# Expert blocks of 128 tokens: 28 tiles of two blocks, then 15 tiles of one block, in a fused two-layer attention and expert kernel

## The reference

```python
# layer 0: E, F, K = 8 experts, 1024 hidden, top 2
probs = softmax(x @ router_w.T); top_w, top_idx = top_k(probs, 2)
top_w = top_w / (sum(top_w) + 1e-9)
h = relu(x @ w1[e].T + b1[e]); y = h @ w2[e].T + b2[e]
out = sum over the two chosen experts of top_w * y
# layer 1: 8 experts, 512 hidden, top 2
h = silu(x @ w1[e]) * (x @ w2[e]); y = h @ w3[e]
out = sum over the two chosen experts of top_w * y
```

## Time and profile before

| | us |
|---|---|
| median of 3 runs | 1743.08 (1738.2 to 1744.42) |
| the profiled execution's own time | 1736.38 |
| its span, first to last instruction | 1734.7 |
| mean granted TensorE clock | 0.927 of 2.4 GHz |
| PE busy | 1543.9 (89%) |
| DVE, ACT, POOL busy | 1095.6, 836.8, 739.2 |

### The profile page before, as it was taken

How to read it: one execution, slowest core, us unless ns; L and a number is a source line. 1 busy time by engine, 2 the same in 40 slices (tenths; PEclk the granted TensorE clock), 3 DMA queues, 4 the chain that set the end, 5 groups by cost and what they waited for, 6 DMA issues and landing times. The chain is left out here.

```text
span 1734.7 us, 38336 instructions
## 1 busy us (share of the span) xinstructions
PE 1543.9 (89%) x12676; PEld 1149.2 (66%) x12676; DVE 1095.6 (63%) x1913; ACT 836.8 (48%) x1548; POOL 739.2 (43%) x521
## 2 busy tenths in 40 slices
PE   7798898897988679999999997999978589999996
PEld 2433334334337568888888885777768579999996
DVE  5687687687778824555554443888868834454443
ACT  2664755655634335555554441666754322322321
POOL 3501303205100036666665442777760046666664
PEclk8899899899895789999999998899995789999999
DMA  6411312213207264555553224200007154443443
GB/s 188 135 56 56 118 61 87 82 61 109 73 25 268 96 232 117 143 144 139 143 145 65 48 44 100 62 25 25 26 2 239 65 159 65 66 68 62 63 65 46
DMA packets 105122, 163.65 MB, mean 94 GB/s; under 512 B 10896, under 2 KB 70340, under 8 KB 104708
## 3 DMA queue, kind: packets, MB, share of 16 engines
q1 hardware_dynamic: 72247, 117.98, 20.8%
q0 software_dynamic: 29952, 40.91, 14.1%
q10 hardware_dynamic: 2791, 2.84, 0.5%
HBM read 92.91 MB, written 68.79 MB: 93 GB/s over the span
## 5 line engine op out<-in xcount | busy, mean ns | idle before, releaser
L1322 PE MATMUL e_ph<-e_zTt,weights_a 128*128 128x256 f16 x3744 | 424.8, 274 | 2.3 <-issue 2.0
L1322 PEld LDWEIGHTS e_ph<-e_zTt,weights_a 128*128 x3744 | 364.6, 98 | 54.0 <-issue 10.7
L1272 POOL DMA_INDIRECT e_zt<-token_parts,slot_token x156 | 172.0, 1103 | 210.3 <-issue 201.9
L1450 DVE TENSOR_TENSOR e_hl<-e_h,e_hh 128x512 f16<-128x512 f32 x156 | 104.4, 690 | 212.0 <-ACT e_hh L1414 189.1
L1400 ACT ACTIVATE e_h<-e_ph,e_b 128x256 f32<-128x256 f32 x312 | 130.6, 470 | 215.6 <-PE e_ph L1322 137.2
L1282 POOL DMA_INDIRECT token_rows<-e_ysb,slot_token x78 | 158.6, 2034 | 173.8 <-DVE e_ysb L1477 159.4
L1336 PE MATMUL e_pyt<-weights_b,e_hh 128*128 x1248 | 210.7, 273 | 0.6 <-DVE e_ysb L1477 0.6
L704 ACT ACTIVATE probs<-lower_banks,shift 128x1024 f32<-128x1024 f32 x128 | 137.3, 1112 | 90.7 <-PE lower_banks L578 89.2
L1282 POOL DMA_INDIRECT out_dram<-e_ysb,slot_token x78 | 124.4, 1595 | 109.2 <-DVE e_ysb L1481 86.5
L1336 PE MATMUL e_pyt<-weights_b,e_hl 128*128 x624 | 170.1, 273 | 0.0
L739 DVE TENSOR_TENSOR acc<-acc,probs 128x1024 f32<-128x1024 f32 (+1 forms) x112 | 136.8, 1222 | 23.6 <-ACT probs L704 20.3
(11 more groups left out here) (233 smaller groups left out, 2867.6 us busy)
## 6 DMA issues: line engine op xcount, KB each, us to landing
weight_parts<-w_split SPq DMA_DIRECT2D x32, 512.0 KB, 3.3
weights_a<-weight_parts SPq DMA_DIRECT2D x16, 1024.0 KB
x_sb<-in_u SPq DMA_DIRECT2D x24, 512.0 KB
weight_parts<-x_sb SPq DMA_DIRECT2D x24, 512.0 KB
w_raw<-in_w1T SPq DMA_DIRECT2D x16, 512.0 KB, 4.5
w_raw<-in_w2T SPq DMA_DIRECT2D x16, 512.0 KB, 4.8
weights_b<-weight_parts SPq DMA_DIRECT2D x8, 1024.0 KB
token_parts<-x_sb SPq DMA_DIRECT2D x8, 1024.0 KB, 5.3
```

Source lines behind the costliest of these rows:

```text
L1272: pool.indirect_dma_start(zt[:, i % 2, c, :], None, g.zrows, at).then_inc(ld[i % 2], 16)
L1322: last = pe.matmul(ph[:, q, f, :], up_w(wp, e, k, 2 * q + f), zTs[:, i % 2, 2 * zp + k, :], start=(n == 0), stop=(n == 5))
L1450: dve.tensor_tensor(hl[:, s, 2 * q:2 * q + 2, :], src[:, q % 2], hh[:, s, 2 * q:2 * q + 2, :], ALU.subtract).then_inc(lo_done, 1)
```

## The change

Each expert's run is padded to 128 slots. `BLOCKS = (2*B*S + E*(P-1)) // P` = 71 blocks stand in place of 78. `PAIRS = 28` tiles of two blocks come first (each expert's even part), then 15 tiles of one block (the odd blocks and what is left), `NT` = 43. `extent(i)` gives a tile's first block, its number of blocks and how many hidden blocks share a PSUM bank.

- A tile of one block makes the same 48 up matmuls, with 128 columns instead of 256, into two banks (alternating between the two halves of `ph`), 4 transposes instead of 8, and one `down` instead of two.
- Its up weights come from `own_w`, two fixed buffers of 1 MB in the upper part of the x buffer. SP's `fetch_own(i)` reads the tile's expert and copies both parts from `weight_parts`. The first two are issued behind `bring_home`, ahead of layer 0's first two `fetch`; each later one waits for the up of the tile two before.
- ACT and DVE work on units of 4 x 128 columns. In layer 0 a unit is four activations of 128 columns. ACT's second loop ends at tile 28, DVE's loop at tile 26; the tiles behind are written out.
- `route` has more steps: pairs and odd blocks are counted and scanned apart, and the expert of each tile comes from two comparisons. One-hot rows shrink from 78 to 71 blocks.

```diff
-NT = (2 * B * S + E * (C * P - 1)) // (C * P)
+BLOCKS = (2 * B * S + E * (P - 1)) // P
+PAIRS = (2 * B * S // P - E) // C
+NT = PAIRS + BLOCKS - C * PAIRS
...
-            step(dve.tensor_scalar(cnti[:], ptot[:, 0:E], float(C * P - 1), None, ALU.add))
-            step(dve.tensor_scalar(cntj[:], cnti[:], (C * P).bit_length() - 1, None, ALU.logical_shift_right))
-            step(dve.tensor_copy(cnt[:], cntj[:]))
-            step(dve.tensor_tensor_scan(cumt[:], g.ones[:, 0:E], cnt[:], 0.0, ALU.mult, ALU.add))
-            step(dve.tensor_tensor(base[:], cumt[:], cnt[:], ALU.subtract))
-            step(dve.tensor_scalar(base[:], base[:], float(C * P), None, ALU.mult))
-
-            step(dve.tensor_tensor(lg[:], prk[:, 0:T * E].rearrange("p (t e) -> p t e", e=E), over_t(base[:]), ALU.add))
+            step(dve.tensor_scalar(cnti[:], ptot[:, 0:E], float(P - 1), None, ALU.add))
+            step(dve.tensor_scalar(blocksi[:], cnti[:], P.bit_length() - 1, None, ALU.logical_shift_right))
+            step(dve.tensor_scalar(pairsi[:], blocksi[:], 1, None, ALU.logical_shift_right))
+            step(dve.tensor_scalar(oddi[:], blocksi[:], 1, None, ALU.bitwise_and))
+            step(dve.tensor_copy(pairs[:], pairsi[:]))
+            step(dve.tensor_copy(odd[:], oddi[:]))
+            step(dve.tensor_tensor_scan(cum_pairs[:], g.ones[:, 0:E], pairs[:], 0.0, ALU.mult, ALU.add))
+            step(dve.tensor_tensor_scan(cum_odd[:], g.ones[:, 0:E], odd[:], 0.0, ALU.mult, ALU.add))
+            step(dve.tensor_scalar(limit[:], pairs[:], float(C * P), None, ALU.mult))
+            step(dve.scalar_tensor_tensor(base[:], cum_pairs[:], float(C * P), limit[:], ALU.mult, ALU.subtract))
+            step(dve.tensor_scalar(away[:], cum_pairs[:], cum_pairs[:, E - 1:E], float(-C * P), ALU.subtract, ALU.mult))
+            step(dve.tensor_tensor(odd[:], cum_odd[:], odd[:], ALU.subtract))
+            step(dve.scalar_tensor_tensor(away[:], odd[:], float(P), away[:], ALU.mult, ALU.add))
+            ranks = prk[:, 0:T * E].rearrange("p (t e) -> p t e", e=E)
+            step(dve.tensor_tensor(wk2, ranks, over_t(limit[:]), ALU.is_ge))
+            step(dve.tensor_tensor(wk2, wk2, over_t(away[:]), ALU.mult))
+            step(dve.tensor_tensor(lg[:], ranks, over_t(base[:]), ALU.add))
+            step(dve.tensor_tensor(lg[:], lg[:], wk2, ALU.add))
...
+            def fetch_own(i):
+                s, b = i % 2, i + PAIRS
+                if i >= PAIRS + 2:
+                    sp.wait_ge(up_done, UB * b - UB)
+                e = expert_of(sp, i)
+                sp.dma_start(own_w[:, s], g.parts[layer][:, :, bass.ds(e, 1), 0:2 * F0].rearrange("p w o n -> p w (o n)")
+                             ).then_inc(own_ld[s], 16)
...
+                if single:
+                    pe.wait_ge(own_ld[s], 16 * ((i - PAIRS) // 2 + 1))
                 pe.wait_ge(zev, i + 1)
-                for q in range(Q):
+                for q in range(UB * cols):
+                    bank = UB * s + q if single else q
...
-                                last = pe.matmul(ph[:, q, f, :], up_w(wp, e, k, 2 * q + f), zTs[:, i % 2, 2 * zp + k, :],
+                                last = pe.matmul(out[:, f, :], up_of(i, e, wp, k, per * q + f), zTs[:, s, 2 * zp + k, 0:cols * P],
...
-                down(i, 0, e[i])
-                if i + 2 < NT:
-                    e[i + 2] = expert_of(pe, i + 2)
-                down(i, 1, e[i])
+                for c in range(extent(i)[1]):
+                    if c == extent(i)[1] - 1 and i + 2 < NT:
+                        e[i + 2] = expert_of(pe, i + 2)
+                    down(i, c, e[i])
```

More of the change, by code:

```diff
@@ L1190, in experts @@
     NF = F // P
[L1191 to L1194, removed]
+    UB = 2
+    HB = UB if layer == 0 else 1
     KINDS = 3
@@ L1233, in experts, with extent, place, landed @@
         up_w, down_w = g.up_w, g.down_w
+        def extent(i):
+            if i < PAIRS:
+                return C * i, C, 2
+            return i + PAIRS, 1, 4
+        def place(x, per):
+            return x.rearrange("p (f t) -> p f t", f=per)
+        def landed(i):
+            return 16 * C * (i // 2) if i < PAIRS else 16 * (i // 2 + PAIRS // 2)
         def expert_of(eng, i):
@@ L1261, in _ @@
                     sp.wait_ge(w_kept[i], 16 * (KINDS * E // 2 + 1))
+            for i in range(PAIRS + 2, NT):
+                fetch_own(i)
             sp.wait_ge(g.w_home[layer], 32 * E)
@@ L1290, in _ @@
                 add_rows(i)
-            for i in range(2):
-                pool.wait_ge(sto[i], 16 * C * ((NT - i + 1) // 2))
+            for i in (NT - 2, NT - 1):
+                pool.wait_ge(sto[i % 2], landed(i) + 16)
         @block.tensor
@@ L1304, in turn, with up_of @@
                 last.then_inc(t_done, 1)
+            def up_of(i, e, wp, k, f):
+                if i < PAIRS:
+                    return up_w(wp, e, k, f)
+                first = g.up_at(k, f)
+                return own_w[:, i % 2, wp, first:first + P]
             def up(i, e):
+                s = i % 2
+                b, cols, per = extent(i)
+                single = i >= PAIRS
                 if i < WATCHED:
@@ L1363, in steps @@
             body(1, 1, True)
-            for first, last in ((1, SPLIT), (SPLIT, NT // 2)):
+            for first, last in ((1, SPLIT), (SPLIT, PAIRS // 2)):
                 with eng.Fori(first, last) as n:
@@ L1384, in _, with body @@
                 act.wait_ge(w_kept[0], 16)
-            def body(i, s, early):
+            def body(i, s, early, single=False):
+                b, cols, per = extent(i) if single else (C * i, C, 2)
                 if layer == 0:
@@ L1398, in units @@
+                    hold(act, g, up_done, UB * b + q + 1)
                     if layer == 0:
-                        for f in range(2):
-                            last = act.activation(h32[:, q % 2, f, :], ph[:, q, f, :], ACT.Relu,
-                                                  bias=b1[:, bass.ds(e, 1), 2 * q + f], scale=1.0 / WS)
+                        for f in range(per):
+                            last = act.activation(place(h32[:, slot], per)[:, f, :], place(ph[:, bank], per)[:, f, :],
+                                                  ACT.Relu, bias=b1[:, bass.ds(e, 1), per * q + f], scale=1.0 / WS)
@@ L1453, in hidden_and_next @@
-            def hidden_and_next(i, s, following, early):
-                gated(i, s, early)
+                for q in range(HB * cols):
+                    slot = s if layer and single else q % 2
+                    dve.wait_ge(hi_done, HB * b + q + 1)
+                    dve.tensor_tensor(hl[:, s, per * q:per * q + per, 0:cols * P], place(src[:, slot], per),
+                                      hh[:, s, per * q:per * q + per, 0:cols * P], ALU.subtract).then_inc(lo_done, 1)
+            def hidden_and_next(i, s, following, early, single=False, next_single=False):
+                gated(i, s, early, single)
@@ L1456, in hidden_and_next, with result @@
                 if layer == 0:
-                    lows(i, s, early)
+                    lows(i, s, early, single)
                 if following:
-                    evacuate(i + 1, 1 - s, False)
+                    evacuate(i + 1, 1 - s, False, next_single)
                 if layer:
-                    lows(i, s, early)
-            def result(i, s, half, early):
+                    lows(i, s, early, single)
+            def result(i, s, half, early, single=False):
+                b, cols, _ = extent(i) if single else (C * i, C, 2)
```

210 lines of the change are left out of this document (117 added, 93 removed).

## The result

| | before | after |
|---|---|---|
| median, us | 1743.75 (1738.2 to 1745.32, 4 runs) | 1721.12 (1718.13 to 1725.87, 4 runs) |
| ratio | | 0.9881, 95% interval 0.9863 to 0.9899 |
| profiled execution / its span | 1736.38 / 1734.7 | 1718.13 / 1716.4 |
| PE busy | 1543.9 | 1490.5 |

The change makes the kernel 22.6 us faster by the medians (1.3%; the ratio says 1.2%), where 44.4 were forecast. The same kernel, run again beside the last experiments, gave 1724.39 (0.9913, 0.9883 to 0.9942). In what follows, up is L1391, turn L1354, down L1407, gather L1321, `add_rows` L1332, `fetch_own` L1284, `evacuate` L1506 and layer 1's result L1562.

The account below looks back on a forecast made before the run. PE was taken to bound both layers, in layer 0 nearly met by a second chain. Layer 0 -25.6, layer 1 -16.4, ends -6.8, route +4.4 gave -44.4 us: 1743.1 to 1699 us, range 1675 to 1733.

Parts of the forecast that it names:

- A pair of load and matmul at 56 ns: PE's up in single tiles: 48 load and matmul pairs at 56 ns each, 2.70 us in all.
- (a): Rival: PE's weight loads overlap only in part, 77 ns each, up takes 3.7 us; 1721 us, chance 0.15.
- (b): Rival: PE's weight loads don't overlap at all, up takes 4.70 us; 1747 us, no gain, chance 0.06.
- Layer 0's copy chain at 6.4: Layer 0's single tiles: activations, casts and DVE's copy hold PE's next up, period 6.4 us; -25.6 us.
- Layer 1's -16.4: Layer 1: 15 single tiles at 5.0 us, set by the weight loads, against 91.4 us for 11 pair tiles.
- POOL comes next: Layer 1: result, rows, then gather to its use 6.6 us, turn and down 1.53; two periods of 4.1, hidden.
- The loads' own period of 5.0: Layer 1: up, expert read and 1 MB landing, 2.70 + 0.6 + 5.3 + 1.4 = 10.0 us for two periods.
- (c): Rival: 1 MB weight loads land late, 12.9 us, 8.1 us per tile in both layers; 1771 us, chance 0.08.
- (d): Rival: PE is never held up, single tiles take 5.54 us in layer 0, 4.23 in layer 1; 1675 us, chance 0.08.
- The clock should hold: PE's clock in the new tiles stays up, with PE busy 87 and 85% of layer 0's and layer 1's periods.
- Ends, -6.8: Ends of the layers: last rows start earlier behind DVE's last result, -4.9 us in layer 1, 1.9 in layer 0.
- Route, +4.4: Route before each layer's tiles: more small steps, shorter one-hot rows; +2.2 us per layer, +4.4 in all.

Follow-up runs that it names:

- experiment 4: Changed kernel without the 1 MB loads; single tiles read `weights_a` through the expert's register, as pair tiles do: 1741.47 us, ratio 1.0.
- experiment 2: Changed kernel with POOL issuing each gather one tile earlier, ahead of the rows of an older tile: 1708.88 us, ratio 0.9823.
- experiment 1: Changed kernel without the 1 MB loads; single tiles read expert 0's weights at a fixed place: 1706.0 us, ratio 0.9799.
- experiment 7: Changed kernel with gathers one tile earlier and no 1 MB loads, expert 0's weights at a fixed place: 1696.34 us, ratio 0.9733.
- experiment 6: Changed kernel with gathers one tile earlier and, in layer 0's single tiles, DVE's copy ahead of `lows`: 1700.64 us, ratio 0.9759.
- experiment 8: experiment 6 with four fixed 1 MB buffers in layer 1 in place of two: 1695.77 us, ratio 0.9723.
- experiment 3: Changed kernel with PE reading the expert ahead of turn for single tiles: 1724.74 us, ratio 0.9879.
- experiment 5: Changed kernel with DVE's copy for the next tile ahead of `lows` in layer 0's single tiles: 1729.32 us, ratio 0.9908.
- experiment 10: experiment 8 plus PE's read of the expert ahead of turn for single tiles: 1699.71 us, ratio 0.9745.
- experiment 9: Changed kernel fetching only the high part of single tiles' up weights, 512 KB, the low part being expert 0's: 1713.92 us, ratio 0.982.
- experiment 11: The changed kernel again, unaltered, beside two later runs: 1724.39 us, ratio 0.9913.

## Why the prediction was right in direction and wrong in size

- **A pair of load and matmul at 56 ns: right.** Up takes 2.67 us, forecast 2.70, so neither (a) nor (b) took place, though (a)'s time, 1721, is the one measured. What the time shares with (a), and nearly with the prediction's estimate of 1726, is an accident; their mark, an up of 3.7 or 3.9 us, is absent. The Trainium skill, TensorE: Matmul & The Clock Gate, section Back-to-back issue gap, has about 81 ns as the sustained rate of such pairs; this case's trace shows 56 over 48 pairs in a row with fixed addresses, and the measurement decides. It shows 85 where addresses are worked out (experiment 4).
- **Layer 0's copy chain at 6.4: right** as a mechanism (6.50 measured; 5.52 once the copy is ahead). 15 tiles were 6.98 in the mean and not 6.4, the stage -21.0 and not -25.6, by late gathers at its start: experiment 2 gets rid of the interval of 10.43.
- **Layer 1's -16.4: the step that failed.** The prediction put it so: "POOL comes next", 6.6 us and then 1.53, "Two periods of 4.1 us: hidden under 5.0". The loop is the right one and was priced too low, at 8.1 us for two tiles in place of 10.58. It takes 5.00 us from a gather's issue to its use and not 3.40, +1.6; the read of the expert, priced at nothing here, stands in the path, +0.46; turn takes 0.40 and not 0.22, and down and result are some 0.2 longer. That gives 5.3 of a period and not 4.1, above the 5.0 of the loads. The first single tiles, with two rows in flight from the pair tiles, cost still more (9.31 at most), and behind the longest waits (2.60 and 2.95 us) the next down runs at the lower clock, 2.5 us in place of 1.3. The stage gained 3.4 us and not 16.4. The prediction had named it as what could make it fail, "if gathers queue behind the 1 MB loads", and gave it no price. Experiments 1, 2 and 7 show both halves of it.
- **The loads' own period of 5.0: borne out in size** by experiment 6 (5.08, landing 6.7), and hidden in the change. It isn't proved to be what binds there, since rows behind rows go at the same pace. That loop the prediction had at 3.96 and called hidden: 4.9 with the loads, 4.3 without.
- **(c), the weights late: no.** They landed in 7.1 us in the median, below the 11.1 from which it decides. **(d)** is what experiments 6 and 7 come near to, layer by layer: 5.52 and 4.21.
- **"The clock should hold": wrong** for single stretches of layer 1, 0.93 in the mean of 1625 to 1675 and 0.50 behind the wait of 2.60 us.
- **Ends, -6.8: too much.** Layer 1's last rows start 1708.06 - 1704.65 = 3.4 us behind DVE's last result, 2.8 earlier than before and not 4.9, since they still wait for the rows before them:

```profile
1704.02 1.55 POOL L1332 DMA_INDIRECT out_dram<-e_ysb,slot_token  x1 [3.83 <-DVE e_ysb L1562]
1708.06 1.55 POOL L1332 DMA_INDIRECT out_dram<-e_ysb,slot_token  x1 [2.49 <-DMA out_dram<-e_ysb,slot_token]
```

  The last two downs start 2.64 us apart (1700.42 and 1703.06), with no up between them; the forecast took them for a period apart. In layer 0 the tail is 0.6 longer, not 1.9 shorter; there it wasn't taken apart.
- **Route, +4.4: near**, +1.3 and +2.4. The small steps cost what the earlier trace rows said, 0.205 us each, as DVE's timeline of the kernel after shows:

```profile
573.80 0.17 DVE L1131 TENSOR_SCALAR e_ei<-e_ptot 128x8 int32<-128x8 f32 x1 [1.22 <-PE e_ptot L999]
574.00 0.17 DVE L1132 TENSOR_SCALAR e_ei<-e_ei 128x8 int32<-128x8 int32 x1
...
576.52 0.42 DVE L1146 TENSOR_TENSOR e_lane_hot<-e_prk,e_e 128x256 f32<-128x256 f32 x1
```

**Open.** Where pair tiles end, a landing of rows takes 4.97 us (experiment 1) and 5.33 (experiment 7) without any load as well, 5.40 in the change; only the next stays long with the loads, 6.17, and falls to 4.20 without (experiment 7). What makes the first of them long was not taken apart. The late intervals vary from one execution to the next, in experiment 8 most of all, and no run says by what. The 1.9 us of the second attention have no cause found.

A part of the spread between executions lies ahead of all that was changed. The first 100 us of two traces, with the columns of the earlier trace rows, of the kernel after and of experiment 3:

```profile
0.00:100.00 100.00, 78.36 (x344) 35.80 (x346) 60.79 (x136) 49.24 (x91) 37.97 (x36) 0.88 0.46 147
0.00:100.00 100.00, 82.11 (x300) 35.12 (x302) 55.04 (x131) 44.21 (x86) 37.67 (x36) 0.74 0.45 140
```

The granted clock is 0.88 here in the traces of the change and of experiments 1, 2, 5, 7 and 10, and their first up of layer 0 starts at 622.2 to 623.8; it is 0.74 to 0.76 in those of 3, 4, 6, 8, 9 and 11, and the first up starts at 628.5 to 632.9. Why was not looked into. So medians of four executions that differ by a few us, as here those of experiments 6, 8 and 10, don't rank two kernels; the periods read inside the stage do not carry this part.

## What to carry to other kernels

When tiles get smaller, every loop that had slack because a tile was long has to be priced again, whole, with its queue order: here a gather stood behind the rows of an older tile, which cost nothing at 8.3 us per tile and set the pace at 5. Price transfers in such a loop under the traffic that the change itself adds, not as they land before it. And take waits away in the order of the loops: the copy's wait removed alone was no gain, and removed after the gather's it was worth 8 us. Then read the chain again: behind both stood rows that wait for rows, which no experiment here took away.

## What the runs showed of the hardware

- Large transfers from HBM lengthen small indirect ones on another queue: a gather of the kernel after lands in 4.9 us in the median (4.6 to 6.2) beside 1 MB loads (1612 to 1690), in 2.8 (2.7 to 4.8) among its pair tiles without them (1400 to 1560), and in 3.82 at one place of experiment 1, whose chain has this:

```profile
1661.75 3.82 DMA e_zt<-token_parts,slot_token
```

  The Trainium skill, DMA: Bandwidth & Descriptors, section Queues, rings and completion order, says that each DMA engine goes round-robin between its queues by the packet. The trace fits that, with 0.78 for the engines' share and 1 to 2 us more per gather; it doesn't show the single packets, so the sharing itself is not shown.
- An address from a register costs the weight load's sequencer 46 ns, 32 times per 48 loads: nothing beside matmuls of 256 columns, 1.41 us per up beside those of 128.
- Behind an idle time of 2.60 us, turn and another 0.46 us, the next 12 matmuls ran at 1.2 GHz (granted clock 0.50).
